# Cross-attention and a routed feed-forward layer: one block per batch for the attention arrays, and another order of keys and weight passes

## The reference

```python
x = x + attention(layernorm(x), ctx, ctx, mask, Wq, Wk, Wv, Wo, bo)
#   qh = q @ Wq;  kh = ctx @ Wk;  vh = ctx @ Wv       (per head)
#   attn = softmax(where(mask, -max, qh @ kh.T / 8));  out = (attn @ vh) @ Wo + bo
x = x + ffn(layernorm(x))
#   scores = sigmoid(x @ gate.T + bias); top 2 of 9, shares normalised to 1
#   out += cw[:, e] * ((silu(x @ w1[e].T) * (x @ w3[e].T)) @ w2[e].T)
```

## Time and profile before

| quantity | value |
|---|---|
| runs | 427.75 us median (427.56 to 428.26) |
| the profiled execution | 428.12 us |
| its span, first to last instruction | 426.3 us |
| PE busy | 404.8 us, 95% |
| DVE, ACT, POOL busy | 277.7, 252.2, 244.9 us |
| bytes moved by DMA | 66.03 MB, 155 GB/s in the mean |

### The profile page before, as it was taken

The page is one execution under the profiler, slowest core; times in us unless marked ns, Lnnn a source line. Parts: engine busy times, 40 slices in busy tenths (PEclk is TensorE's granted clock), DMA queues, the critical chain, the costliest instruction groups (busy, mean ns, idle before and its releaser), DMA issues.

```text
span 426.3 us, 10134 instructions
## 1 busy us (share of the span) xinstructions
PE 404.8 (95%) x3176; PEld 307.6 (72%) x3176; DVE 277.7 (65%) x684; ACT 252.2 (59%) x443; POOL 244.9 (57%) x213
## 2 busy tenths in 40 slices
PE   8899899999999999786999999999999999999991
PEld 8677577788877887674677777777777777777771
DVE  1777889899899989979688955444444444444340
ACT  3759889999899948444556444444444444444430
POOL 6536879998998865444054535445444444544242
PEclk9999999999999999989899999999999999999997
DMA  8992356566575624438767998888999888988753
GB/s 266 364 325 62 123 148 207 161 181 197 158 235 162 184 82 158 144 113 175 162 119 133 148 137 130 137 145 139 139 144 144 143 143 142 123 144 149 116 77 37
DMA packets 106241, 66.03 MB, mean 155 GB/s; under 512 B 80977, under 2 KB 99281, under 8 KB 106193
## 3 DMA queue, kind: packets, MB, share of 16 engines
q1 hardware_dynamic: 98512, 54.90, 55.2%
q0 software_dynamic: 7680, 10.49, 16.0%
HBM read 36.23 MB, written 9.96 MB: 108 GB/s over the span
## 4 chain that ended last, share of the span: by engine, by line
PE 58%; issue 16%; DMA 9%; DVE 6%; POOLq 3%; POOL 3%; ACT 2%; DVEq 0%; ACTq 0%
PE ps L816 14%; PE ps L648 12%; PE ps L618 11%; DMA out_rows<-work,idx_all 9%; PE ps L836 7%; PE ps L631 4%; POOLq L1707 3%; POOL work L1698 3%; PE ps L520 2%; PE ps L613 2%; PE ps L587 1%; PE ps L664 1%; PE ps L532 1%; DVE work L1136 1%; PE ps L602 1%
## 5 line engine op out<-in xcount | busy, mean ns | idle before, releaser
L816 PE MATMUL ps<-w_all,work 128*128 x960 | 151.4, 314 | 2.3 <-issue 2.3
L816 PEld LDWEIGHTS ps<-w_all,work 128*128 128x128 f16 x960 | 94.3, 99 | 48.9 <-issue 2.4
L1719 POOL DMA_INDIRECT out_rows<-work,idx_all x40 | 64.1, 1602 | 105.2 <-ACT work L1073 101.8
L1511 DVE SCALAR_TENSOR_TENSOR work<-ps,work 128x352 f32<-128x352 f32 x80 | 41.3, 523 | 66.9 <-PE ps L816 66.8
L836 PE MATMUL ps<-w_all,work 128*128 x681 | 80.8, 273 | 0.0
L836 PEld LDWEIGHTS ps<-w_all,work 128*128 128x128 f16 x681 | 66.4, 98 | 10.7 <-issue 0.2
L1636 POOL TENSOR_TENSOR w_all<-stage,w_all 128x1088 f16<-128x1088 f32 x30 | 67.6, 2256 | 9.2 <-ACT w_all L910 8.6
L1052 ACT ACTIVATE work<-ps 128x352 f32<-128x352 f32 x80 | 36.8, 463 | 54.0 <-PE ps L816 53.9
L1058 ACT ACTIVATE work<-work 128x704 f16<-128x704 f32 x39 | 30.8, 790 | 62.4 <-DVE work L1511 62.4
L1698 POOL DMA_INDIRECT work<-xn_rows,idx_all x40 | 41.2, 1029 | 29.0 <-issue 10.2
L618 PE MATMUL ps<-w_all 128*128 128x462 f16 (+1 forms) x288 | 57.4, 336 | 0.0
(11 more groups left out here) (159 smaller groups left out, 537.9 us busy)
## 6 DMA issues: line engine op xcount, KB each, us to landing
stage<-in_wt SPq DMA_DIRECT2D x36, 544.0 KB, 4.5
work<-in_x SPq DMA_DIRECT2D x30, 128.0 KB, 3.6
out_rows<-work SPq DMA_DIRECT2D x18, 128.0 KB, 4.4
xn_rows<-work SPq DMA_DIRECT2D x18, 128.0 KB, 4.4
w_all<-in_x SPq DMA_DIRECT2D x1, 1536.0 KB, 14.7
work<-work SPq DMA_TRANSPOSE x78, 3.7
w_all<-in_wk SPq DMA_DIRECT2D x2, 512.0 KB, 5.2
w_all<-in_wq SPq DMA_DIRECT2D x4, 256.0 KB, 7.0
```

Source lines behind the costliest of these rows:

```text
L816: mm = pe.matmul(ps[:, c, 0:half], xt[:, t % 2, block, :], weights(wbase + off, half), start=(k == 0 and n == 0), stop=(k == KD - 1 and n ...
L1511: dve.scalar_tensor_tensor(out=sg[:, t % 2, cols], in0=ps[:, 2 + c, 0:HID // 2], scalar=1.0 / SP_W, in1=sg[:, t % 2, cols], op0=ALU.mult, ...
L1719: pool.indirect_dma_start(out=acc, out_offset=bass.IndirectOffsetOnAxis(ap=idx_all[:, t:t + 1], axis=0), in_=yb[:, t % 2], in_offset=None, ...
```

## The change

**Layout.** The arrays `a_hi`, `a_lo`, `maskb` and `b_hi` of one batch now form one block of 8104 two-byte elements per partition, and the two blocks follow each other. The block of batch 0 is no longer read once the scores and products of tiles 0 to 7 are over, and expert 7's chunks 28 to 30 fall into room that is free by then.

**Weight passes.** Chunks 28, 29 join the two-chunks-a-step pattern in step 14, chunk 30 is done in step 15 (all three by ACT's two passes and POOL), chunks 31 and 32 by ACT and DVE in the drain. The loads on SP move with them: 34 and 35 now stand ahead of the expert stage.

**Start.** 30 warm matmuls in place of 40; Wk comes in three parts (cut at pairs 2 and 4); SP waits for the second before it issues x; PE runs keys 0 to 4, then alternates `key_side` with keys 5 to 7.

**Smaller moves.** `b_high(3)` before `exp(1)` and `b_low(3)`, `b_low(4)` earlier; ten warm matmuls before `first_turn`; `gate_copy(13)` before `first_high`; on DVE `normalise2(15)`, `shares(0)` and `logits` placed elsewhere in the first expert tiles; `store_xn2(15)` behind `turn_tokens(2)` on SP.

```diff
+        A_BLK, M_BLK, B_BLK = KD * HJ, TPB * J, NCH * D
+        BLOCK = 2 * A_BLK + M_BLK + B_BLK
+        blocks = late[:, 0:B * BLOCK].rearrange("p (b n) -> p b n", b=B)
...
-        WARM, WARM_IDS, WARM_OUT = 40, 30, 16
+        WARM, WARM_IDS, WARM_OUT, WARM_X0 = 30, 30, 16, 10
...
-        W_LAST = W_STEP + 2 * EARLY - W_PRE // 2
+        W_LAST = W_STEP + 2 * EARLY - W_PRE // 2 + 1
...
+        K_CUTS = (0, 2, 4, PAIRS)
...
-            for g in range(2):
-                sp.dma_start(wk_sb[:, :, g * half:(g + 1) * half],
...
+            for g in range(3):
+                cols = slice(K_CUTS[g] * P, K_CUTS[g + 1] * P)
+                sp.dma_start(wk_sb[:, :, cols], wk[:, cols].rearrange("(k p) n -> p k n", p=P)).then_inc(wk_in[g], 16)
...
                 if g == 0:
+                    sp.wait_ge(wk_in[1], 16)
                     load_x_all(0)
... SP, step(n)
+                if n == NT - 1:
+                    load_w(4 * EARLY + 3)
...
+                if n == NT:
+                    load_w(4 * E9 - 3)
...
-                if n == W_LAST:
-                    load_w(4 * EARLY)
-                    load_w(4 * EARLY + 1)
-                if n == W_LAST + 1:
+                if n == NT - 2:
                     load_w(4 * EARLY + 2)
+                if n == NT - 1:
+                    load_w(4 * E9 - 4)
 
             for n in range(NT + 1):
                 step(n)
-            load_w(4 * EARLY + 3)
             store_x1(NT - 3)
-            load_w(4 * E9 - 4)
             store_xn2(NT - 4)
             store_x1(NT - 2)
             store_xn2(NT - 3)
-            load_w(4 * E9 - 3)
+            load_w(4 * E9 - 2)
+            load_w(4 * E9 - 1)
... SP, fstep(n)
                     store_x1(NT - 1)
                     store_xn2(NT - 2)
+                if n == 0:
                     store_xn2(NT - 1)
-                    load_w(4 * E9 - 2)
-                if n == 1:
-                    load_w(4 * E9 - 1)
... PE
                     if i == NT - 1 and c == X0_AT:
+                        warm(WARM_X0, WARM_LATE)
                         first_turn()
... ACT, step(1), step(15), drain
                     w_high(W_PRE - 1)
+                    b_high(3)
                     exp(1)
-                    b_high(3)
                     b_high(4)
...
-                    for c in range(2):
-                        w_scale(4 * EARLY + c)
-                    act.wait_ge(sc_mm, 3 * NT)
-                    for c in range(2):
-                        w_round(4 * EARLY + c)
+                    w_high(4 * EARLY + 2)
...
-            for c in range(2, 4):
-                w_direct(4 * EARLY + c)
+            w_direct(4 * EARLY + 3)
+            w_direct(4 * E9 - 4)
...
+            gate_copy(NT - 3)
             first_high()
-            gate_copy(NT - 3)
... DVE, drain and fstep(n)
-                w_rest(4 * EARLY + 2)
+                w_rest(4 * EARLY + 3)
+                w_rest(4 * E9 - 4)
...
                     normalise2(NT - 2)
-                    w_rest(4 * EARLY + 3)
+                if n == 0:
+                    normalise2(NT - 1)
                     shares(0)
-                    normalise2(NT - 1)
-                if n in (1, 2):
-                    logits(NT - 3 + n)
                 if n == 1:
-                    w_rest(4 * E9 - 4)
                     held_of(0)
                 if n == 2:
+                    logits(NT - 1)
...
                     first_values()
+                    logits(NT - 2)
... POOL, step(n)
                 if n == NT - 1:
-                    w_low(4 * EARLY)
+                    w_low(4 * EARLY + 2)
                 if on(n, LAG_X1):
                     rstd(n - LAG_X1)
-                if n == NT - 1:
-                    pool.wait_ge(s16_ok, 1)
-                    w_low(4 * EARLY + 1)
```

More of the change, by code:

```diff
@@ L536, in key_side, with keys @@
                             mm.then_inc(a_mm, 1)
+            def keys(m):
+                pe.wait_ge(wk_in[sum(m >= c for c in K_CUTS[1:])], 16)
+                at_least(pe, k_ok, m - 3)
+                head_values(wk_sb, m, K_BANKS[m % 4])
             def value_side(m):
+                pe.wait_ge(k_ok, PAIRS)
                 pe.wait_ge(wv_in[m // (PAIRS // 2)], 16)
@@ L591, in _ @@
             pe.wait_ge(ctx_in, 16)
-            for m in range(PAIRS):
-                pe.wait_ge(wk_in[m // (PAIRS // 2)], 16)
-                at_least(pe, k_ok, m - 3)
-                head_values(wk_sb, m, K_BANKS[m % 4])
             def norm_turn(i):
@@ L777, in drain @@
                 gate_logits(NT - 3)
+            for m in range(5):
+                keys(m)
             for m in range(3):
                 key_side(m)
+                keys(m + 5)
+            key_side(3)
             value_side(0)
-            key_side(3)
+            value_side(1)
+            key_side(4)
+            value_side(2)
             pe.wait_ge(con_in, 16)
             norm_turn(0)
-            value_side(1)
-            for m in range(4, PAIRS):
+            for m in range(5, PAIRS):
                 key_side(m)
@@ L884, in v_even, with k_copy @@
                                ACT.Copy).then_inc(v_half[0], 1)
-            for m in range(PAIRS):
+            def k_copy(m):
                 act.wait_ge(kv_mm, m + 1)
@@ L1013, in key_pair @@
                 a_high(2 * m + 1)
-            act.wait_ge(vz_ok, 1)
+            for m in range(5):
+                k_copy(m)
             for m in range(3):
                 key_pair(m)
+                k_copy(m + 5)
+            key_pair(3)
+            act.wait_ge(vz_ok, 1)
             v_even(0)
+            v_even(1)
             normalise(0)
-            key_pair(3)
-            v_even(1)
+            key_pair(4)
+            v_even(2)
             normalise(1)
             x_high(0)
-            for m in range(4, PAIRS):
+            for m in range(5, PAIRS):
                 key_pair(m)
@@ L1404, in step @@
             def step(n):
+                if n == 2:
+                    b_low(4)
                 if on(n, 1):
@@ L1411, in step @@
                     stats1_of(4, 6)
-                if n == 2:
-                    b_low(4)
                 if on(n, LAG_OUT):
@@ L1432, in step @@
                 if n == 1:
+                    b_low(3)
                     stats1_of(6, 8)
                     aggregate1(2)
-                    b_low(3)
                     dve.wait_ge(bc_in, 32)
@@ L1473, in drain @@
                 aggregate(NT - 2)
-                w_rest(4 * EARLY + 2)
+                w_rest(4 * EARLY + 3)
+                w_rest(4 * E9 - 4)
                 first_low()
                 logits(NT - 3)
+            a_low(0)
+            dve.wait_ge(xall_in[0], 16)
+            stats1_of(0, 2)
+            aggregate1(0)
+            for m in range(1, 3):
+                a_low(m)
+            a_low(3)
             dve.wait_ge(vz_ok, 1)
-            for m in range(3):
-                a_low(m)
             v_odd(0)
-            a_low(3)
             v_odd(1)
+            a_low(4)
+            v_odd(2)
             x_low(0)
-            for m in range(4, PAIRS):
+            for m in range(5, PAIRS):
                 a_low(m)
```

50 lines of the change are left out of this document (19 added, 31 removed).

## The result

The changed kernel takes 423.89 us (median of 4 runs, 422.82 to 424.05). The kernel before, run beside it, takes 428.0 us (427.56 to 430.62). The ratio is 0.990, 95% interval 0.985 to 0.994. It is faster, as forecast, and inside the range of 418.5 to 425.0, but 2.9 us above the 421.0 that was given. Two later sets of six runs of it gave 423.25 and 422.98. The profiled execution took 422.82 us with a span of 421.0, against 426.3: 5.3 less where 6.7 was forecast.

What follows compares the result with a forecast made beforehand. PE was taken as full in the token loop and from 210 us, so the time lay in its waits and slow clock. -1.3 - 1.7 - 3.7 = -6.7 from 428.12 gave 421.4, median 421.0; range 418.5 to 425.0.

Steps and rivals of the forecast that it cites:

- Term 1: Start: fewer warm matmuls and reordered keys bring the first scores at 21.5 against 22.80, -1.3 us.
- this backlog hides SP's delay: Start: transfers already lag their issue, so SP's wait should not make constants, Wv or mask late; no cost.
- the 7.9 for the first `key_side`: Start: the first key-side product was taken to begin at 7.9 us, between 7.5 and 8.4.
- rival B: Start gives nothing since Wk and Wq bind PE: 1.3 us less gain, 422.3 us; chance 0.12.
- Term 2: Steps 1 and 2: `b_low(4)` ends earlier, so scores of step 2 start at 46.2: -1.7 us.
- Token loop: Two more chunks in step 14 with PE full: costed at nothing, 0.5 us if ACT's `gate_copy` came late.
- Term 3: Drain: ten warm matmuls cost 0.6 us, `gate_copy` gives back about 0.35, so `up(0)` is +0.3 us.
- Term 4: Expert tiles 0 to 3: earlier tile 2 transpose, no long stall, full clock; `ranks(1)` -3.7 us with Term 3 inside.
- A: Expert stage: the wait moves to tile 1's transpose, behind chunk loads 34 and 35: +3.6 us, 424.6; chance 0.12.
- C: Drain: PE's clock does not fall, `first_turn` 1.6 us earlier, 1.4 of it left: 419.6 us; chance 0.10.
- those for "wrong": PE waiting for Wk or Wq, DVE or ACT late in steps 3 to 14, `up(1)` after 191.6, among others.
- those for "right": First scores at 21.5 (20.8 to 22.0), clock 1.0 through `up(2)`, no DMA landing ahead of a PE wait, among others.

Runs made afterwards that it cites:

- the unchanged kernel: The changed kernel run once more with no edit: 423.25 us, ratio to the kernel before 0.985.
- spread loads: Against the changed kernel, chunk 34 loads behind expert tile 0's last xn2 store, chunk 35 behind tile 3's transpose: 421.62 us, repeated 421.89.
- the run with POOL beside DVE: Against the changed kernel, POOL's last `w_low` in step 15 waits for DVE's subtraction of tile 15: 425.99 us.

## Why the prediction came out as it did

**Term 1, start, -1.3: failed.** Two steps failed. The one reads "this backlog hides SP's delay". It does not: SP issues x at 5.40 and Wv 2.15 us later than before, the DMA engines move 185 GB/s where they moved 369, and PE waits for Wv, 0.72 us in the first profile and 0.55 to 1.89 in seven of the nine later ones with this start. The other is the 7.9 for the first `key_side`. I took it from the landings of a Wk in two parts (and my own row of terms, 4.8 and five pairs at 0.55 and half a us, gives 8.05); the third part lands at 7.8, but pair 4 of the keys has to be made after it, so it starts at 8.7. In the first profile the two waits (0.33 and 0.72) are 1.05 of the missing 1.2 us. In the second one there is no wait for Wv and 1.18 us for Wk. So which transfer is late changes from one execution to the next. That SP's hold itself costs time is not shown: without it the kernel was no faster, and with Wv ahead of x it was no faster either. What the runs show is rival B's outcome: the new start is worth 0.1 us, and its first scores come at 22.9 in the middle of ten profiles where I had 21.5.

**Term 2, steps 1 and 2, -1.7: right.** -1.6 in the trace, and +1.4 us (0.4 to 2.4) in the time when undone.

**Token loop, 0: right.** It lost 0.14 us over some thirteen steps, with two more chunks in it.

**Term 3, drain, +0.3: wrong in sign, by a mechanism not foreseen.** I wrote that the change takes nothing from DVE until `first_low`. One DVE row was 0.8 us shorter in the changed kernel, since POOL's `w_low` of step 15 was over, and another 0.2 us shorter; with it the wait ahead of `project(14)` fell from 2.10 to 1.33. The warm matmuls gave back part, 16 of them at the lower clock 0.16. That the row waits for POOL's pass is shown, by the run that makes them collide; that this is the whole gain of the drain is argued from one trace of each kernel.

**Term 4, expert tiles 0 to 3: right in mechanism, and 0.4 us short of the forecast.** `up(2)` came at 197.12 where 196.1 was forecast, `ranks(1)` at 207.74 for 206.7. Seen from `up(0)`, 19.68 us for 19.4. The wait ahead of `ranks(1)` is not there: DVE's row for it ends at 207.39, before PE is through with `up(3)`. In its place PE waits 1.08 us ahead of `down(0)` for the transpose of the hidden rows, which come late from DVE since the gather for tile 2 is late. With the whole order undone the stall of 2 us came back, and 1.8 us (0.5 to 3.0) in the time.

**The rivals.** A and C came both, and each hides the other. C, the full clock in the drain, was there in seven of the later profiles (16 warm matmuls in 1.05 us), but what it gives at `up(0)` is taken at `up(1)` by A's wait for tile 1's transpose: 1.85 us in the unchanged kernel's second profile, behind which the clock stayed at 1.00. So A's cost depends on C. With the drain at the lower clock, `up(0)` to `ranks(1)` takes 19.68 and 19.78 us in the changed kernel and 18.89 and 19.38 in the two such profiles with spread loads; at the full clock it takes 21.4 to 21.8 in four profiles with the two loads ahead, and 18.67 and 20.77 in the two with spread loads. In time the spread loads show about 1.0 us, where A was priced at 3.6. The prediction priced A and C one at a time; a chain in which an earlier start meets a transfer that does not come earlier with it has no sum of the two.

**The time.** The five terms left the span 1.4 us above the forecast (start +1.2, steps 1 and 2 +0.1, loop +0.1, drain -0.8, expert tiles +0.4, end +0.3, rounded). I had put the median 0.37 below the profiled execution, as it was before; here it was 1.07 above it. Together that is the 2.9 us. That the time came out inside the range owes something to luck: 0.8 us from a DVE row that I had not looked at stand against the 1.2 that the start did not give. Undone one at a time, the start, the order around step 2 and the order of the expert stage cost 0.1, 1.4 and 1.8 us, 3.3 of the 4.1 us by which the kernel got faster.

**The signs.** Of those for "wrong", two came: PE waited for Wk, and `up(1)` started at 192.06 where 191.6 was the limit. Of those for "right", the first scores missed their window, and a DMA landed ahead of a wait of PE at `down(0)`. PE had no wait in steps 3 to 14, and its clock was 1.00 from `up(0)` through `up(2)`, as stated.

## What to carry to other kernels

Before a queue is held back to protect one transfer, ask who is waiting for the last transfer behind it, and look at the rate in the windows after: here the engines fell to 185 GB/s, and PE waited for Wv. When loads are moved out of a late place, look at what they stand ahead of in the new one: here a load next to a small transpose or gather that an engine waits for cost it 1 to 4 us of landing. And before a gain upstream is added to the sum, find the next event that does not move with it.

## What was not expected of the hardware

- A DVE `tensor_scalar` of nine float32 elements per partition, from SBUF to SBUF, took 0.21 us with POOL idle, and 1.02 and 1.80 us when a POOL pass ran; both times it ended within 0.03 us of the pass. The rows around it (a reduce, operations with a PSUM operand, `reciprocal`) were not held.
- The same program has the clock at 1.2 GHz or at 2.4 GHz in the drain from one execution to the next: 16 warm matmuls took 1.05, 1.73 and 1.87 us in three profiles of the changed kernel. In two kernels and at the same place a wait of 2.10 us was followed by no fall and one of 2.09 us by a granted clock of 0.50. At the start the waits of 1.62 and 1.89 us were followed by a granted clock of 0.50, and one of 1.48 was not. What decides it stays open.
- A transpose that took 2.4 to 2.8 us with no load near it (once 3.8, issued 0.2 us behind a gather) took 5.2, 5.9 and 6.2 us with a load of 544 KB issued half a us to one us before it. With two such loads it took 3.7 and 4.0 us when they were issued 2 to 4 us before, and 5.4 when they were issued 1 to 2.5 us before (the run with POOL beside DVE).
- The start is not the same from one execution to the next. Ten profiles with the start of the changed kernel have their first scores between 22.24 and 24.86 us. What differs is what PE waits for Wk and Wv, and PE's pace: in the latest one it had the granted clock at 0.50 for three us behind the wait for Wv, and in the next, at 23.48, the 20 matmuls of the first five pairs took 4.87 us with no wait inside, where another profile had 3.43. The column of the granted clock reads 1.00 in those windows, and also where warm matmuls take 107 ns, so at the very start the pace is better read from the durations.
